# GpSimd multiplies units 10 and 12 instead of 9 and 11, with a changed order of the first step: a Mamba block and a mixture of experts on one core

## The reference

```
dt = softplus(dt @ W_dt.T + b_dt);  A = -exp(A_log)
h = h * exp(dt_t[:, :, None] * A) + (dt_t * u_t)[:, :, None] * B_t[:, None, :]
y = einsum('bdn,bn->bd', h, C_t)
y = (y + xc * D) * silu(z);  out = y @ W_out.T
```

## Time and profile before

| | |
|---|---|
| median of 3 runs | 2156.39 us (2154.66 to 2159.53) |
| the profiled execution | 2157.32 us, span 2155.6 us |
| VectorE busy | 1952.6 us, 91% |
| TensorE busy | 1869.6 us, 87% |
| GpSimd busy | 1809.0 us, 84% |
| ScalarE busy | 1528.4 us, 71% |
| stage of the scans | from about 75 to 1679 us |
| DMA | 265.32 MB, mean 123 GB/s |

### The profile page before, as it was taken

One profiled execution on the slowest core, in us unless ns is written; L12 is line 12 of the kernel. 1 busy time (PEld: TensorE's weight loads), 2 busy tenths in 40 slices (PEclk: granted clock), 3 DMA queues, 4 the chain that ended last, 5 costly groups with the idle time before them and its releaser, 6 DMA issues.

```text
span 2155.6 us, 26056 instructions
## 1 busy us (share of the span) xinstructions
PE 1869.6 (87%) x6376; PEld 791.4 (37%) x6377; DVE 1952.6 (91%) x1814; ACT 1528.4 (71%) x3148; POOL 1809.0 (84%) x624
## 2 busy tenths in 40 slices
PE   7889897988889897989888898989774799999997
PEld 3323232323233332323232333323221466655554
DVE  7989999999999999999999999999999777557776
ACT  5787879788888879776888888887866333434443
POOL 5699999999999999999999999999999333415444
PEclk9989898989989898989898998989886899999999
DMA  6754535353535544453536354454434642335444
GB/s 261 248 141 125 129 105 127 102 129 102 144 97 126 122 116 117 112 130 101 127 102 149 94 132 108 115 124 113 108 92 134 243 177 79 109 80 81 77 78 69
DMA packets 140347, 265.32 MB, mean 123 GB/s; under 512 B 21264, under 2 KB 44048, under 8 KB 139072
## 3 DMA queue, kind: packets, MB, share of 16 engines
q1 hardware_dynamic: 125488, 242.05, 41.4%
q0 software_dynamic: 13440, 17.93, 4.9%
q10 hardware_dynamic: 1296, 3.93, 0.5%
HBM read 194.51 MB, written 70.39 MB: 123 GB/s over the span
## 4 chain that ended last, share of the span: by engine, by line
DVE 26%; ACT 20%; PE 18%; issue 17%; POOL 6%; DMA 6%; DVEq 3%; SPq 2%; POOLq 0%; ACTq 0%
DVE hst L1610 15%; ACT psum L1257 8%; DVE dbu L1589 6%; PE psum L2186 5%; POOL hst L940 3%; PE psum L2030 3%; POOL dbu L928 3%; PE psum L2198 3%; DMA dtu_scratch<-dt 3%; ACT dbu L1289 2%; DMA bc_scratch<-sp_tmp 1%; DVEq L1852 1%; DVE h L1862 1%; DMA out_x<-h,target_u 1%; DVE h L1874 1%
## 5 line engine op out<-in xcount | busy, mean ns | idle before, releaser
L940 POOL TENSOR_TENSOR hst<-hst,c_rep 128x2048 f32<-128x2048 f32 x254 | 1145.2, 4538 | 5.5 <-ACT state L1243 5.5
L1610 DVE TENSOR_TENSOR_SCAN hst<-psum,state,dbu 128x1024 f32<-128x1024 f32 x384 | 878.8, 2333 | 19.8 <-ACT psum L1257 19.8
L1257 ACT ACTIVATE psum<-dt_rep,neg_a 128x512 f32<-128x512 f32 (+1 forms) x1024 | 660.6, 676 | 154.0 <-DVE hst L1610 152.4
L1589 DVE TENSOR_TENSOR dbu<-psum,b_rep 128x2048 f32<-128x2048 f32 x176 | 399.2, 2268 | 5.4 <-PE psum L2015 5.4
L928 POOL TENSOR_TENSOR dbu<-dtu_rep,b_rep 128x2048 f32<-128x2048 f32 x80 | 363.4, 4543 | 11.9 <-DVE hst L1610 11.8
L1610 DVE TENSOR_TENSOR_SCAN hst<-psum,dbu 128x1024 f32<-128x1024 f32 x128 | 285.6, 2273 | 12.1 <-ACT psum L1257 12.1
L2030 PE MATMUL psum<-hst,same 128*32 128x512 f32 x2048 | 267.4, 669 | 30.3 <-POOL hst L940 25.0
L2015 PE MATMUL psum<-dt,same 32*128 32x512 f32 x352 | 212.9, 686 | 90.0 <-DVE dbu L1589 79.6
L1962 PE MATMUL psum<-xp,taps 128*128 128x512 f32 x512 | 234.2, 600 | 12.4 <-ACT sp_tmp L1226 10.2
L1050 POOL DMA_INDIRECT out_x<-h,target_u x72 | 112.8, 1567 | 153.2 <-DMA out_x<-h,target_u 79.3
L1996 PE MATMUL psum<-sp_tmp,w_dt 16*128 16x512 f32 x128 | 92.6, 836 | 87.5 <-ACT sp_tmp L1211 69.1
(11 more groups left out here) (186 smaller groups left out, 2496.8 us busy)
## 6 DMA issues: line engine op xcount, KB each, us to landing
dt_rep<-dt_scratch SPq DMA_DIRECT2D x256, 256.0 KB, 4.8
dtu_rep<-dtu_scratch SPq DMA_DIRECT2D x320, 64.0 KB, 1.9
taps<-taps_scratch SPq DMA_DIRECT2D x64, 256.0 KB, 3.6
b_rep<-bc_scratch SPq DMA_DIRECT2D x64, 256.0 KB, 4.9
c_rep<-bc_scratch SPq DMA_DIRECT2D x64, 256.0 KB, 7.8
dt_scratch<-dt SPq DMA_DIRECT2D x63, 256.0 KB, 4.9
h<-slot_scratch SPq DMA_DIRECT2D x72, 129.5 KB
sp_tmp<-t_scratch SPq DMA_DIRECT2D x16, 512.0 KB, 6.8
```

Of the source, the lines that this page charges most:

```text
L940: nc.gpsimd.tensor_tensor(h, h, c_rep[q % 2][:], ALU.mult).then_inc(prod_done, 1)
L1257: nc.scalar.activation(psum[:, PS_A + i, kept], dt_rep[:, G % 2, j, kept], ACT.Exp, scale=neg_a[:, q % 2, u, i:i + 1]).then_inc(exp_done, 1)
L1589: nc.vector.tensor_tensor(dbu[:, U % DBU, :, :], psum[:, PS_U:PS_U + 1, :].broadcast_to((P, NG, TB)), b_rep[U // UNITS % 2][:], ALU.mult). ...
L1610: nc.vector.tensor_tensor_scan(both(hst[:, U % RING, groups, :]), both(psum[:, PS_A + 2 * pair:PS_A + 2 * pair + 2, :]), both(dbu[:, U % D ...
```

## The change

GpSimd's units 9 and 11 become 10 and 12, so VectorE multiplies 9 and 11. The spreadings on TensorE, the waits and SyncE's list follow this. In step 0 three more things move: SyncE's store of the modulation table behind the four loads of the first decay rows, TensorE's projection `project_x(1, 0)` in front of the first two spreadings, and its `convolve(1, 2)` from T = 2 to T = 3; and ScalarE's softplus of the next step's chunks 0, 1 and 2 goes to later places (`FIRST_DT_AT`).

```diff
-FIRST_DT_AT = [(10, 0), (10, 3), (12, 0), (13, 1)]
+FIRST_DT_AT = [(10, 3), (11, 3), (12, 1), (13, 1)]
-POOL_UNITS = (3, 7, 9, 11, 15)
+POOL_UNITS = (3, 7, 10, 12, 15)
@@ SyncE, before the steps
             spread_rows(0)
+            spread_dt(0, 0)
             sp.wait_ge(mod_step, 6)
             sp.dma_start(mod_dram, mod[:, :, 2:6, :]).then_inc(mod_stored, 16)
-            spread_dt(0, 0)
@@ SyncE, in each step
-                spread_dtu(q, 9)
+                spread_dtu(q, 10)
                 if q + 2 < STEPS:
                     load_xnT(q + 2)
-                spread_dtu(q, 11)
                 if q == 0:
                     store_dt(0, 3)
+                spread_dtu(q, 12)
                 spread_dt(q, 3)
@@ ScalarE, softplus
-                    act.wait_ge(u_full, vector_mults(UNITS * (q - 1) + GN * c + 2))
+                    act.wait_ge(u_full, vector_mults(UNITS * (q - 1) + GN * c + GN - 1))
@@ TensorE, spread_input
-                if j == 0:
+                if j == 0 or (j == 1 and on_pool(U - 1)):
                     pe.wait_ge(dtu_done, G + 1)
@@ TensorE, before the units
+            project_x(1, 0)
             spread_input(0)
-            project_x(1, 0)
             spread_input(1)
@@ TensorE, in each unit
-                if (t == 9 and q > 0) or (t == 13 and ahead) or T == 5:
+                if t == 8 or (t == 13 and ahead) or T == 5:
                     spread_input(T + 3)
-                if 0 < T < ALL_UNITS - 2 and not on_pool(T + 2) and T != 6 and (t != 10 or q == 0) and t != 14:
+                if 0 < T < ALL_UNITS - 2 and not on_pool(T + 2) and T != 6 and t != 9 and t != 14:
                     spread_input(T + 2)
                 if T == 2:
                     project_x(1, 3)
-                    convolve(1, 2)
                     turn_xn(6, 0)
                 if T == 3:
+                    convolve(1, 2)
                     convolve(1, 3)
```

## The result

| | before | after |
|---|---|---|
| median of 20 runs each | 2159.69 us (2154.66 to 2161.89) | 2162.19 us (2159.49 to 2163.76) |
| ratio | | 1.0014, 95% interval 1.0008 to 1.0021 |
| the profiled execution | 2157.32 us, span 2155.6 us | 2162.73 us, span 2161.0 us |

The kernel after is 0.14% slower (3.0 us by the ratio): less than the 0.2% that the prediction called no change, but clear of one. The prediction was 2156.0 us and a step of -0.4 us. The 6.2 us between 2156.0 and 2162.2 are two things: 2.9 us of change that it hadn't priced (2.5 by the medians, where it said -0.4; 3.4 by the ratio), and 3.3 us because more runs of the kernel before have a median of 2159.7, not of 2156.4.

The account below looks back on a forecast made before the run. VectorE's gap at unit 8 sets the seeded step (100.0 us), with GpSimd's 99.2 us floor just below. Terms -8.1 + 7.7 + 1.1 - 1.1 = -0.4 us gave 2156 us, range 2148 to 2165.

Parts of the forecast that it names:

- Term 1: Units 10 and 12, steps 1 to 15: GpSimd's waits for scans go, -8.1 us.
- Term 2: Step 0: unit 12's row, made late, stalls GpSimd and delays SyncE's queue up to the next step's dt, +7.7 us.
- Term 3: Start of step 0: projection in front delays spreading 1, +1.1 us (+0.3 to +2.0); convolution, store and softplus moves zero.
- Term 4: End of the last step: VectorE, which ends the stage, may come closer to GpSimd, -1.1 us.
- A: Step 0: the loss eats only GpSimd's cover towards VectorE, so the 8.1 us gain stays; 2148 us, chance 0.20.
- B: SyncE's queue behind multiply 10 makes GpSimd wait before the next step's product in every step; 2168 us, chance 0.14.
- C: ScalarE stops VectorE at units 12 and 13 instead of 8, steps stay at 100.0 us; 2164 us, chance 0.08.
- D: A denser VectorE slows GpSimd's operations, all weighings at their upper end; 2180 us, chance 0.03.

Follow-up runs that it names:

- b_steady_units: The kernel before with units 10 and 12 on GpSimd from step 1 on only, step 0 unchanged; 2150.78 us, ratio 0.9963 to the kernel before.
- a_early_product: The kernel after with GpSimd's product of chunk 3 in step 0 one weighing sooner; 2159.23 us, ratio 1.0002 to the kernel before.
- b_swap_all: The kernel before with units 10 and 12 on GpSimd in all steps, nothing else of the change; 2157.37 us, ratio 0.9995 to the kernel before.
- before_again: The kernel before, unchanged, run once more for a second profile; 2160.05 us in one run.
- a_px_conv_back: The kernel after with both the projection and convolve(1, 2) back in their old places; 2157.18 us, ratio 0.9991 to the kernel before.

## Why the prediction was wrong, step by step

- **What bounds the kernel**: right. GpSimd's floor of 99.2 us a step, and its lateness paid to the end. From multiply 3 of step 1 to the end of GpSimd's weighings it is 1478.2 to 1480.2 us in all fourteen profiles with the new units in the later steps, while the first of these points lies anywhere between 192.4 and 205.6; of 13 us of lateness 1 or 2 at most are made up.
- **Term 1** (-8.1): right. -8.0 us in b_steady_units, and the stretch just named is 1487.3 to 1488.6 us in the three profiles with the old units, 8.8 more in the mean.
- **Term 2** (+7.7): right. 6.9 us by the times, 7.1 to 8.2 in the timelines, with its two stalls at 4.88 and 4.26 us; making the row of unit 12 sooner takes the first away (a_early_product).
- **Term 3** (+1.1): here it failed, with 4.1 us in its place (the kernel after against b_swap_all, 1.0014 against 0.9995; 4.9 at the end of GpSimd's weighings). Two parts of it:
  - The convolution was put at nothing, since ScalarE's copy of the last turned tile waited for TensorE "with convolutions (1,2) and (1,3) both ahead of it, and they are still ahead". True, but the turned tile between them waits for ScalarE's normed tile, and the convolution fills that wait. It was moved from in front of a wait to behind it, and what this costs is the length of the wait: 1.88 us of idle TensorE, 2.1 us on GpSimd, 0.9 to 3.0 us in three pairs of times. The prediction's own trace was no help: there the convolution waited for its taps, and the move would have looked free in it.
  - The projection in front was worked out only up to spreading 1, which came out in its range (79.32; 78.1 to 79.8 forecast), for +0.3 to +2.0 us. In five pairs of times it cost 0.6 to 4.3 us, 2.8 in the mean, so this size is less sure than the convolution's. The working looked at when the projection's bank is free, and not at what it left behind: TensorE idle for 2.58 us while VectorE multiplies unit 0, which the projection had filled. It took one execution's timing of spreading 1 for the kernel's, too, though the stretch from L1996 to spreading 1 is 10.8 us in that trace and 9.5 in before_again, against 13.0 in the kernel after.
  - The half clock adds to what is seen between the first two traces, and not to the price of the change. The working had a half clock for the projection alone. Spreading 1 took 2.07 us and not 1.12, so that GpSimd's first multiply came 2.46 us later than in the first profile of before and not 1.51, and from spreading 1 to the third it was 8.4 us and not the 4.7 of the earlier trace rows; but before_again and the other kernels with the projection in its old place have this too.
  - The store and the softplus places, both at zero: right.
- **Term 4** (-1.1): didn't come. VectorE did end its last scan 1.0 us closer to GpSimd (it starts at 1680.38, 4.08 late, where GpSimd is 5.05 late), but its next instruction took 1.0 longer. This is told below.
- **The profile it stood on**: the first execution of before had an early return to full clock at the start and a wait for taps, together worth 1.5 us at the end, and lay in the lower of two groups of times. The prediction was made from the median of three runs, 2156.4; twenty give 2159.7. This moved the predicted time, though not the predicted step.

With the measured terms the sum is -8.0 + 6.9 + 4.1 = +3.0 us. The first two come from b_steady_units and b_swap_all; the third is what is left to the kernel after, so the sum can't fail to close. What supports it is that its two pieces, measured by themselves (2.8 us in the mean of five pairs, 1.9 in the mean of three), make 4.7 us, which is the same within the error, and that with both taken back (a_px_conv_back, 0.9991) nothing is left above b_swap_all (0.9995).

**Rivals.** A (loss in step 0 hidden) was refuted by b_swap_all. B (queue behind multiply 10) happened once, 0.7 us. C (the gap moves to units 12 and 13) was refuted by steps of 99.2 to 99.3 us with VectorE's waits for decays down from 25.6 to 9.8 us between 190 and 1680 us (9.1 us of waits for TensorE are new). D (a denser VectorE slows GpSimd): GpSimd's weighings have a median of 4526 ns, against 4534 before. The outcome was none of the four: it was the forecast's own term 3, of which the range knew an upper end of 2.0.

## What to carry to other kernels

When an instruction is moved on an engine that waits now and then, ask of both places whether it stood inside a wait: as much of an instruction as fills a hole is free there, and moved elsewhere it costs that much more (here 1.9 us of a 3.6 us convolution), even if everything it was ahead of stays behind it. Look for this in more than one execution, since a rare wait can cover the hole. Price a moved start down to the next point where the other engines meet it, and not just to the first instruction behind, and compare at the same granted clock on both sides. And if a change is good in all steps but the first, because the first one's inputs are made later, make it for the others alone: here the units alone, from step 1 on and with none of the other moves, made -8.0 us where the whole change made +3.0.
